# Score matmuls on 64-row tiles with a masking matmul, in place of full-height tiles with zero-padded keys

## What is computed

```python
# B, S, E = 16, 512, 128;  H, KVH = 16, 4;  D = 8;  QL, KVL = 64, 32;  F = 352
xn = layernorm(x)
q  = rope((xn @ Wqa @ Wqb).reshape(B, S, H, D))
kv = (xn @ Wkva @ Wkvb).reshape(B, S, KVH, D, 2)
k, v = rope(kv[..., 0]), kv[..., 1]            # each of the 4 serves 4 heads
scores = einsum('bqhd,bkhd->bhqk', q, k) * D ** -0.5, -inf where key > query
a  = softmax(scores) @ v @ Wout + bout
ffn(xn) = fp4_linear(silu(fp4_linear(xn, w_gate)) * fp4_linear(xn, w_up), w_down)
out = x + a + ffn(xn)                          # fp4: blocks of 16, quantized and back
```

## Time and profile before

| | |
|---|---|
| runs | 964.93, 965.22, 1162.7 us; median 965.22 |
| profiled execution | span 971.2 us, first to last instruction; no other time is given for it |
| busy | TensorE 798.9, VectorE 745.1, GpSimd 580.3, ScalarE 546.6 us |
| mean granted TensorE clock | 0.948 |
| DMA | 58.5 MB, mean 60 GB/s |

### The profile page before, as it was taken

One profiled execution on the slowest core, in us unless ns is written; L12 is line 12 of the kernel. 1 busy time (PEld: TensorE's weight loads), 2 busy tenths in 40 slices (PEclk: granted clock), 3 DMA queues, 4 the chain that ended last, 5 costly groups with the idle time before them and its releaser, 6 DMA issues.

```text
span 971.2 us, 22358 instructions
## 1 busy us (share of the span) xinstructions
PE 798.9 (82%) x6782; PEld 494.7 (51%) x6861; DVE 745.1 (77%) x1636; ACT 546.6 (56%) x1105; POOL 580.3 (60%) x624
## 2 busy tenths in 40 slices
PE   3367878889897988979797997978889897989886
PEld 1234545646464554646455564645646464565544
DVE  4899788797977878787886879778797978878600
ACT  1123566646665664645665565565656656666672
POOL 3344665657665665657656475755677576566541
PEclk9596999999999999979999899998999999999998
DMA  4312121212222121221212222130222222121000
GB/s 124 107 56 76 46 76 41 65 50 85 59 84 51 49 74 32 85 61 59 73 48 58 51 84 59 52 79 15 84 59 85 58 58 74 38 69 28 24 22 11
DMA packets 66278, 58.47 MB, mean 60 GB/s; under 512 B 17298, under 2 KB 56178, under 8 KB 66170
## 3 DMA queue, kind: packets, MB, share of 16 engines
q1 hardware_dynamic: 66170, 57.04, 21.8%
HBM read 31.81 MB, written 18.61 MB: 52 GB/s over the span
## 4 chain that ended last, share of the span: by engine, by line
PE 41%; DVE 28%; issue 14%; POOL 6%; ACT 6%; another core or an unknown queue 2%; DVEq 1%; SPq 1%; DMA 0%; POOLq 0%; ACTq 0%
DVE neg_max L627 10%; PE pv_ps L1019 9%; DVE xn L712 6%; PE exp_ps L1001 6%; PE max_ps L986 5%; PE misc_ps L1086 5%; POOL P L489 4%; PE misc_ps L1037 4%; PE misc_ps L1047 3%; DVE m_split L641 2%; PE max_ps L987 2%; ACT P L853 2%; PE misc_ps L1055 2%; PE misc_ps L1084 2%
## 5 line engine op out<-in xcount | busy, mean ns | idle before, releaser
L627 DVE TENSOR_REDUCE neg_max<-max_ps 128x1 f32<-128x512 f32 (+3 forms) x768 | 432.2, 595 | 139.6 <-PE max_ps L987 130.5
L853 ACT ACTIVATE P<-exp_ps 128x512 f32<-128x512 f32 x512 | 294.5, 603 | 247.3 <-PE exp_ps L1001 127.0
L986 PE MATMUL max_ps<-K,Q 128*128 128x384 bf16 (+2 forms) x768 | 203.6, 284 | 47.9 <-DVE neg_max L627 25.5
L1001 PE MATMUL exp_ps<-Q,K 128*128 128x384 bf16 (+3 forms) x945 | 219.6, 300 | 19.0 <-ACT P L853 15.6
L987 PE MATMUL max_ps<-Kd,Q 128*128 128x128 bf16 x1024 | 194.2, 225 | 2.4 <-DVE neg_max L627 1.3
L1019 PE MATMUL pv_ps<-P,V 128*32 128x512 f32 (+3 forms) x2048 | 166.5, 444 | 12.4 <-POOL P L489 5.2
L489 POOL TENSOR_SCALAR_AFFINE_SELECT P<-P 128x512 f32<-128x512 f32 x256 | 154.1, 636 | 19.2 <-ACT P L856 19.2
L986 PEld LDWEIGHTS max_ps<-K,Q 128*128 128x128 bf16 x768 | 77.2, 101 | 132.9 <-DVE neg_max L627 68.0
L987 PEld LDWEIGHTS max_ps<-Kd,Q 128*128 128x128 bf16 x1024 | 101.4, 101 | 43.2 <-issue 20.0
L1001 PEld LDWEIGHTS exp_ps<-Q,K 128*128 128x128 bf16 x1024 | 82.9, 100 | 59.0 <-ACT P L853 34.1
L856 ACT ACTIVATE P<-exp_ps 128x512 f32<-128x512 f32 x128 | 77.6, 606 | 44.1 <-PE exp_ps L1001 43.8
(11 more groups left out here) (110 smaller groups left out, 1155.3 us busy)
## 6 DMA issues: line engine op xcount, KB each, us to landing
Q<-q_scr SPq DMA_DIRECT2D x64, 224.0 KB
q_scr<-q_split SPq DMA_DIRECT2D x16, 384.0 KB, 2.4
Kd<-K SPq DMA_DIRECT2D x64, 96.0 KB
x_in<-x SPq DMA_DIRECT2D x16, 256.0 KB, 2.8
q_scr<-q_split SPq DMA_DIRECT2D x16, 256.0 KB, 2.7
x_res<-x SPq DMA_DIRECT2D x16, 256.0 KB, 5.2
out<-y SPq DMA_DIRECT2D x16, 256.0 KB, 3.8
K<-k_scr SPq DMA_DIRECT2D x64, 48.0 KB
```

Of the source, the lines that this page charges most:

```text
L627: nc.vector.tensor_reduce(neg_max[:, i, h0:h0 + len(heads)], max_ps[r % 3][:, 0:len(heads) * n].rearrange("p (h k) -> p h k", k=n), AX.X, ...
L853: nc.scalar.activation(P[g % 2][:, hh + r % 2, col:col + 512], ps[:, :], ACT.Exp, scale=SCALE).then_inc(exp_done, 1)
L986: nc.tensor.matmul(ps[:, col:col + d], Qt, Kt[:, half, g, 0:d], start=True, stop=True)
L1001: last = nc.tensor.matmul(exp_ps[n % 2][:, col:col + width], K[par][:, half, pr // 2, kb * 128:(kb + 1) * 128], Q[par][:, pr, kb * 128:S], ...
```

## The change

Each score matmul uses only the 64-row half of its head: 48 partitions for the maxima, 50 (`EROW`) for the exponentials. `K` loses its index of halves and its zeros. `Kd`, `mask_k`, `mask_q`, the seventh slot of Q and `copy_k` go. The causal mask of the maxima's diagonal blocks becomes a second matmul, which adds the product of two constant 64 x 128 tiles to the same PSUM columns. GpSimd makes these tiles at the start. The tables of tiles give in each slot one maximum tile in one half and the next exponential tile in the other. Its place in a pair of slots (`pr % 2`) decides which head of each half it works on (`2 * g + x`); the blocks of 256 queries and keys are all in even slots, those of 128 in odd ones.

```diff
+EROW = MROW + 2
+MASK_STEP = 40
-LOAD_K, LOAD_Q, COPY_K = 6, 2, 2
+LOAD_K, LOAD_Q = 6, 2
-MAX_TILES = [((0,), 3), ((1,), 3), ((0,), 2), ((1,), 2), ((0, 1), 1), ((0, 1), 0)]
+MAX_TILES = [
+    [(0, (0,), 3), (1, (0,), 3), (0, (0,), 2), (1, (0,), 2), (0, (0, 1), 1), (1, (0, 1), 1)],
+    [(0, (1,), 3), (1, (1,), 3), (0, (1,), 2), (1, (1,), 2), (1, (0, 1), 0), (0, (0, 1), 0)],
+]
...
 EXP_TILES = [
-    [(0, 0, 0)], [(1, 0, 0)],
-    [(0, 1, 0), (0, 3, 384)], [(1, 1, 0), (1, 3, 384)],
-    [(0, 2, 0), (1, 2, 256)],
+    [(1, [(0, 0, 0)]), (0, [(0, 0, 0)]), (1, [(0, 1, 0), (0, 3, 384)]), (0, [(0, 1, 0), (0, 3, 384)]),
+     (1, [(0, 2, 0), (1, 2, 256)])],
+    [(1, [(1, 0, 0)]), (0, [(1, 0, 0)]), (1, [(1, 1, 0), (1, 3, 384)]), (0, [(1, 1, 0), (1, 3, 384)]),
+     (0, [(0, 2, 0), (1, 2, 256)])],
 ]
...
-        K = [sb(f"K{i}", [128, 2, KVH, S], BF16) for i in range(2)]
-        Kd = sb("Kd", [128, 2, KVH, S], BF16)
+        K = [sb(f"K{i}", [128, KVH, S], BF16) for i in range(2)]
...
-        N_CONST_DMA = 14
+        N_CONST_DMA = 4
...
-                                  ap=[[E * S, NSLOT + 1], [NPAIR * S, D], [1, NPAIR // 2 * S]])
-                    sp.dma_start(Q[i][r:r + (NSLOT + 1) * D, 4 * hf:4 * hf + 4, :], src).then_inc(qk_loaded[hf], 16)
-
-            def copy_k(T, hf):
-
-
-                T.wait(sp, k_loaded[hf], 16 * LOAD_K, 2, 16 * LOAD_K)
-                T.wait(sp, max_filled, NPAIR * NMAX, 1, (hf + 1) * NPAIR // 2 * NMAX)
-                for half in range(2):
-                    r, gs = HALF * half, slice(2 * hf, 2 * hf + 2)
-                    sp.dma_start(Kd[r:r + MROW, half, gs, :], K[i][r:r + MROW, half, gs, :]).then_inc(qk_loaded[hf], 16)
+                                  ap=[[E * S, NSLOT], [NPAIR * S, D], [1, NPAIR // 2 * S]])
+                    sp.dma_start(Q[i][r:r + NSLOT * D, 4 * hf:4 * hf + 4, :], src).then_inc(qk_loaded[hf], 16)
...
+                nc.gpsimd.memset(mask_a_sb[:, :], 0.0).then_inc(masks_set, 1)
+                nc.gpsimd.memset(mask_b_sb[:, :], 0.0).then_inc(masks_set, 1)
+                select(mask_a_sb, ALU.not_equal, 0, 2.0 ** MASK_STEP, 2)
+                select(mask_a_sb, ALU.not_equal, 1, 2.0 ** -MASK_STEP, 3)
+                select(mask_a_sb, ALU.not_equal, -128, 2.0 ** MASK_STEP, 4)
+                select(mask_a_sb, ALU.not_equal, 1 - 128, 2.0 ** -MASK_STEP, 5)
+                select(mask_b_sb, ALU.is_ge, 1 - 128, -2.0 ** (2 * MASK_STEP), 6)
+                pool.wait_ge(masks_set, 7)
+                nc.gpsimd.memset(mask_b_sb[0:HALF, :], 0.0).then_inc(masks_set, 1)
+                select(mask_b_sb, ALU.is_ge, 1, -2.0 ** (2 * MASK_STEP), 8)
+                select(mask_b_sb, ALU.not_equal, 1, -1.0, 9)
+                select(mask_b_sb, ALU.not_equal, 1 - 128, -1.0, 10)
...
-            for k in (K[0], K[1], Kd):
-                nc.vector.memset(k[:, :, :, :].bitcast(F32), 0.0).then_inc(k_zeroed, 1)
...
             def max_tile(T, pr, r):
...
-                heads, i = MAX_TILES[r]
+                a, xs, i = MAX_TILES[pr % 2][r]
...
-                Kt, ps, g, n = K[T.par(1)], max_ps[r % 3], pr // 2, (i + 1) * 128
-                Qt = Q[T.par(1)][:, pr, i * 128:n]
-                for a, half in enumerate(heads):
-                    col, d = a * n, i * 128
-                    if i > 0:
-                        nc.tensor.matmul(ps[:, col:col + d], Qt, Kt[:, half, g, 0:d], start=True, stop=True)
-                    last = nc.tensor.matmul(ps[:, col + d:col + n], Qt, Kd[:, half, g, d:n], start=True, stop=True)
+                ps, g, d, n = max_ps[r % 3], pr // 2, i * 128, (i + 1) * 128
+                half, lo = slice(HALF * a, HALF * a + MROW), HALF * a
+                for k, x in enumerate(xs):
+                    nc.tensor.matmul(ps[:, k * n:k * n + n], Q[T.par(1)][half, 2 * g + x, d:n], K[T.par(1)][half, g, 0:n],
+                                     start=True, stop=False)
+                    last = nc.tensor.matmul(ps[:, k * n + d:k * n + n], mask_a_sb[lo:lo + HALF, :], mask_b_sb[lo:lo + HALF, :],
+                                            start=False, stop=True)
                 last.then_inc(max_filled, 1)
...
             def exp_tile(T, pr, r):
...
-                for half, kb, col in EXP_TILES[r]:
+                a, parts = EXP_TILES[pr % 2][r]
+                half = slice(HALF * a, HALF * a + EROW)
+                for x, kb, col in parts:
                     width = S - kb * 128
-                    last = nc.tensor.matmul(exp_ps[n % 2][:, col:col + width], K[par][:, half, pr // 2, kb * 128:(kb + 1) * 128],
-                                            Q[par][:, pr, kb * 128:S], start=True, stop=True)
+                    last = nc.tensor.matmul(exp_ps[n % 2][:, col:col + width], K[par][half, g, kb * 128:(kb + 1) * 128],
+                                            Q[par][half, 2 * g + x, kb * 128:S], start=True, stop=True)
```

More of the change, by code:

```diff
@@ L149, in sem @@
             return ctx.enter_context(nc.semaphore(name))
-        q_scr = [nc.dram_tensor(f"q_scr{i}", (NSLOT + 1, E, S), BF16).ap() for i in range(2)]
+        q_scr = [nc.dram_tensor(f"q_scr{i}", (NSLOT, E, S), BF16).ap() for i in range(2)]
         k_scr = [nc.dram_tensor(f"k_scr{i}", (3, KVH * D, S), BF16).ap() for i in range(2)]
@@ L354, in _ @@
                                      w[r0:r0 + rn * rows, :].rearrange("(c p) k -> p c k", p=rn)).then_inc(weights_in, 16)
[L356 to L374 removed]
+            for i in range(2):
+                for half in range(2):
+                    r = HALF * half + MROW
+                    sp.dma_start(K[i][r:r + 2, :, :],
+                                 ones16[:, :].rearrange("r (g t) -> r g t", g=KVH)).then_inc(const_dma, 16)
             sp.wait_ge(const_dma, 16 * N_CONST_DMA)
```

65 lines of the change are left out of this document (27 added, 38 removed).

## The result

| | before | after |
|---|---|---|
| median of the runs | 968.18 us | 1000.52 us |
| span of the profiled execution | 971.2 us | 999.5 us |
| mean granted TensorE clock | 0.948 | 0.905 |
| TensorE busy | 798.9 us (82%) | 826.0 us (83%) |

The changed kernel is slower: ratio 1.0351, 95% interval 1.0304 to 1.0398, over its four runs (997.5 to 1009.8 us) and those of the kernel before without the one of 1162.7 us, which was in a slow state of the chip. The forecast was 962.

A forecast was written before the change was run, and what follows sets the result against it. TensorE (82% busy) and VectorE (77%) were taken to share the end. A 35 us saving against 29 us for shape changes, taken as -3 us on 965.2, gave 962 us, range 925 to 1045.

The forecast's parts named there:

- Side by side: Score tiles: matmuls on the two row halves overlap, masks included, saving 4.8 us per batch.
- Changes of shape: At misc jobs between 64-row scores: 28 added tile-shape changes per batch at 0.13 us, costing 3.6 us per batch.
- The reach: Score blocks: 46% is on the chain, so 35 us of saving reaches the end, against 29 us for shape changes.
- rival 4: TensorE: lower granted clock, or dearer row changes; one more 6 us half-speed stretch per batch, 96 us, 1060 us; chance 0.05.
- The sum of -3 us: Whole kernel: net effect taken between -6 and +6 us, giving 962 us from 965.2.
- Kd, "nothing": Loads: removing four Kd copies and one of seven Q-load slots per batch gains nothing, the first-half copy having 19 us slack.
- The start, VectorE and ScalarE, zero: Program start: GpSimd's new work fits its 7.76 us wait, zero; reductions and exponentials unchanged, zero within 0.1 us.

The follow-up runs named there:

- e10: Changed kernel with two 64-column constant matmuls, at 128 then 64 rows, ahead of the first misc job at 16 places a batch: 1024.43 us.
- e11: Changed kernel with two 64-column constant matmuls, both at 128 rows, ahead of the first misc job at 16 places a batch: 1003.05 us.
- e5: Kernel before, with the first four exponential tiles of each pair of heads at 50 rows and maxima still at 128: 1023.35 us.
- e7: Kernel before, with the first four tiles of each pair at 64 rows for maxima and 50 for exponentials, masked K kept: 984.79 us.
- e9: Changed kernel with constant 128-row matmuls added only in the first batch of maxima and the last batch of exponentials: 996.34 us.
- e14: Changed kernel with GpSimd waiting for VectorE's xn ahead of its operation on h, so neither this nor x_bias runs beside xn: 957.39 us.
- e15: Kernel before, with GpSimd waiting for VectorE's xn ahead of its operation on h: 928.51 us.
- e8: Changed kernel with 14 constant matmuls a batch around the turn of each batch, at 64 rows instead of 128: 1003.98 us.

## Why the prediction was wrong, by its steps

- **Side by side, -4.8 us per batch:** right in mechanism, contrary to program order, and right in size at the place named (0.60 us for the first four tiles and their masks, forecast 0.48 without the change of shape; before 0.88, where the prediction had 0.85). TensorE's recorded work in slots 3 to 7 fell by 0.8 us (28.56 to 27.74).
- **Changes of shape:** the gap of 0.09 us is as read from the earlier trace rows. With half of it on the path I had 29 us for 28 x 16 changes at 0.13 us; e10 against e11 gives 28 x 16 x 0.042 = 19.
- **The reach, "46% of the saving":** mis-sized. For slots 3 to 7, 5/8 of a batch, I had 3.0 us of saving, masks included, and 1.4 of it at the end. At the full clock they took 0.1 us more than before (31.19 for 31.09 in the mean of 12 batches), with 17 of the 28 changes of shape in them, 17 x 0.04 = 0.7 us. So by this estimate the tiles themselves gave 0.7 - 0.1 = 0.6 us, a fifth. Scaled to 16 whole batches that is 15 us for my 35, against 19 for my 29 of shape: +4 where I had -6. The share of a line on the chain says how often it is last, not that a cut of it comes out whole: VectorE was busy for 23 to 24 of these 31 us, and its idle time before the reductions grew all the same (151.2 us, 139.6 before). By itself this would have left the kernel within 2%, as forecast; that the two errors nearly cancel is luck.
- **The clock, left out of the sum (rival 4, chance 0.05):** the step that failed. The sum of -3 us has the matmuls at the clock of the kernel before; the clock went from 0.948 to 0.905 instead, and where it is low the edited and the unedited matmuls are slower. I had the effect (16 stretches of 6 us), and saw in the earlier trace rows that the clock is low where TensorE had idled. I didn't see that the change takes rows out of the array in every score matmul, in a kernel that has idle places in slots 0 and 1. The price of a stretch was mis-sized: 89 us more at the lower level cost not 89 but at most 32 us, 0.36 per us. In the last batch it was (44.1 - 36.9) / (2 x 0.19 x 44.1) = 0.43. A reason may be, and isn't shown, that a matmul that is slower while TensorE would wait for ScalarE anyway costs nothing.
- **Kd, "nothing":** the copies were worth nothing to the loads, as said, but they delayed x_res, the transfer queued behind them. xn grew from 67.8 us over the program to 70.8: 3 us. I had asked who waits for the removed copies, not who is queued behind them.
- **The start, VectorE and ScalarE, zero:** right; the reductions kept their 432 us and the first maximum started at 42.2 against 41.7 us.

Of the 28 us between the two traces (32 between the medians):

| where | us | what the runs show |
|---|---|---|
| slots 0 and 2, 13 batches | 8.6 | most of it comes with the lower clock: at the full clock both are as long as before, in the same trace |
| last batch's exponentials | 7.2 | goes with rows and clock by e5 to e7; 4.0 us given back in e9 |
| slot 1, 13 batches | 5.5 | the wait for xn, some 3 us of it by x_bias, and the clock (e14, e15); not divided |
| first batch's maxima | 4.2 | goes with the rows of the maxima; the clock isn't shown to be the way |
| slots 3 to 7, 13 batches | 1.3 | at the full clock |
| elsewhere at the ends | 1.5 | not looked for |

So about half of the loss is tied to the lower clock by rows of its own, and slot 1 adds to it. That rows of the array, and not TensorE's shorter time in work, lower the clock rests on e8 alone and isn't fully separated.

## What to carry to other kernels

A change that puts less of the array to work in each matmul can lower the granted clock for everything on TensorE, as it did here. Before spending a saving there, look for the places where TensorE already waits, and compare the granted clock window by window, and the same slot at either level: a group that nobody edited and that got longer (pv, 444 to 485 ns) is the sign. Don't take a share of the chain for the part of a cut that comes out at the end; slots in which a second engine is busy for three quarters of the time returned about a fifth of the saving where the share said 46%. When a transfer is removed, follow the next one in its queue to the engine that it feeds: one wait that kept GpSimd away from VectorE's xn was worth 40 us, more than the whole question about the tiles.
